# Hand-over between two fused graph networks: the last residual sums of the first network go to other buffers and its last steps to later places

## The chip, the cores and the metric

The kernel runs on one core of a Trainium2 chip. The metric is the device time of one execution in microseconds (us). Before the change it is 1732.25 us, the median of three runs (1732.20 to 1734.21).

## The reference

`x` holds 128 graphs of 64 nodes with 384 features (8192 rows), `adj` the 128 adjacency matrices of 64 x 64. Two networks run one after the other, each of two layers, and each is closed by a residual sum and a layer norm without gain:

```
x = layernorm(x + L0(x, adj))      # gated network
x = layernorm(x + L1(x, adj))      # softmax network

L0, per layer: u = h Wl' h' (row >= column side) or h Wr' h' (other side), / sqrt(H)
               att = exp(u) * adj / (row sum + 1e-10);  ctx = att (h Wlin' + b)
               h = relu((ctx - mean) / (std + 1e-3) * a + b2)
L1, per layer: a = softmax(h h' / sqrt(H)) * adj, rows divided by their sums
               ctx = (a upper)(h Wl' + bl) + diag(a) (h Ws' + bs) + (a lower)(h Wr' + br)
               h = relu((ctx - mean) / sqrt(var + 1e-12) * g + beta)
```

Every product of TensorE is made of three: each operand is split into a high and a low part, and high x high, high x low and low x high are summed.

## The kernel before

**Tiling.** The rows are worked off in 8 passes of two streams (s = 0, 1); a stream is four tiles of 128 rows, and a tile holds two graphs. A pass has four units: unit 0 and 1 are layer 0 of stream 0 and 1, unit 2 and 3 are layer 1 of stream 0 and 1. The first network does its 8 passes and writes its result to the array `x1` in HBM, then the second does its 8 from there. Each engine has its own instruction list, in an order written out by hand; semaphores are the only link, so an instruction that waits holds everything behind it on its engine. The first and the last pass of each network are unrolled, and the unrolled last pass of the first network already starts the second one.

**A unit of the second network.** TensorE folds the scores (`fold_parts`, L1128 and L1131), computes twelve value products V0 to V11 (`values`, L1155, nine matmuls each, in a ring of four PSUM banks), the scores of the next unit (L119) and the contexts (L1168). V_j with j mod 3 below 2 needs its bank to be seeded with the bias by ScalarE (`seed`, L1254), and the seed needs the bank to have been read by VectorE (`biased_value` of job j-4, L1492 or L1496; for V0 and V1 of the first unit of all, `context_stats` of the first network, L761). ScalarE copies the high parts (`value_hi`, L1260), VectorE subtracts the low parts. In units 2 and 3 TensorE also transposes the exponentials (L1139), and while units 1 and 2 run it transposes the rows of units 2 and 3 (`turn_block`, L1112).

**The hand-over.** The results of the last units of the first network stand in `z[0]` and `z[1]`. For both streams there are still to come, in this order: gain and shift (`gain_and_shift`, VectorE L793 and L796), the residual sum (`add_residual`, L803, z and x_res to z), the row statistics of the sum (`final_stats` L808, `final_var` L812 to L817), the power -0.5 on GpSimd (`final_roots`, L634), the offset (`final_offset`, L821), the normalisation on ScalarE (`final_normalise`, L509) and the store to `x1` on the SP queue (`store_last`, L312). Before the change this stands at:

- stream 0: residual sums and statistics in VectorE's last `up_to_contexts` of the first network, ahead of `context_stats`; the roots on GpSimd ahead of the gated roots of stream 1; the four normalisations (`gated_normalise(0)`) in ScalarE's list of unit 0, between `seed` 6 and `value_hi` 3; the store on SP, ahead of the first weights of the second network's second layer (L1049).
- stream 1: gain and shift, sum and statistics in VectorE's list of units 0 and 1; roots on GpSimd in unit 0; normalisations on ScalarE in the second half of unit 1.

Layer 1's weights of the second network (three, staged in the second network's `x_res` buffers) are split in high parts (`weight_hi`, ScalarE L1207) and low parts (`weight_lo`, GpSimd L1371). The third one is loaded once the first is split, and the first rows `x_res` of the second network once all three are.

Of the kernel before, what the change touches and what calls it, by code (L numbers as in the profile page):

```python
# [123 lines left out]
def gated_layers(nc, ctx, sh, x, x_t, adj, adj_t, w_left, w_right, w_lin_t, b_lin, ln_a, ln_b, table, x1,  # L124
# [26 lines left out]
    with ExitStack() as overlaid:  # L151
# [14 lines left out]
        x_res1 = late("x_res1", [P, NT, H])  # L166
# [16 lines left out]
        x_res = [sb("x_res0", [P, NT, H]), x_res1]  # L183
# [66 lines left out]
        def sync_program(sp):  # L250
# [91 lines left out]
            def store_last(s):  # L342
                store_x1(PASSES - 1, s)
# [104 lines left out]
        def scalar_program(act):  # L448
# [136 lines left out]
            def last_normalise(s):  # L585
                final_normalise(PASSES - 1, s)
# [105 lines left out]
        def vector_program(dve):  # L692
# [151 lines left out]
            def up_to_contexts(i, unit, last, s):  # L844
# [23 lines left out]
                if not more:  # L868
                    add_residual(i, s)
# [3 lines left out]
                if more:  # L873
                    query_lo(i, unit + 1, 0)
                context_stats(i, unit, 0, more)
                if s is not None:
                    final_stats(i, s, NT - 1)
                context_stats(i, unit, 1, more)
                if s is not None:
                    final_var(i, s)  # L880
                context_stats(i, unit, 2, more)
                context_stats(i, unit, 3, more)
# [18 lines left out]
            class Tail:  # L901
# [12 lines left out]
                @staticmethod  # L914
                def residual_and_stats(tiles):
                    add_residual(*end, tiles)
                    for t in tiles:
                        final_stats(*end, t)

                @staticmethod  # L920
                def final_var():
                    final_var(*end)

                @staticmethod
                def final_offset():
                    final_offset(*end)
# [6 lines left out]
def softmax_layers(nc, ctx, sh, gated, x1, adj_t, w_nbr_t, table, out):  # L933
# [26 lines left out]
    with ExitStack() as block_ctx:  # L960
# [84 lines left out]
        def _(sp):  # L1045
# [15 lines left out]
            store_last(0)  # L1061
# [4 lines left out]
            store_last(1)  # L1066
            sp.wait_ge(split, SIDES)

            def one_pass(i, last):
# [21 lines left out]
            one_pass(0, False)  # L1091
# [109 lines left out]
        def _(act):  # L1201
# [84 lines left out]
            def second_half(i, unit, more, tail):  # L1286
# [11 lines left out]
                if tail:  # L1298
                    gated_normalise(1)
# [7 lines left out]
                if tail:  # L1307
                    weight_hi(2)
                if more:
                    copy_part(i, unit + 1)  # L1310

            def one_pass(i, last, first=False):

                for unit in range(UNITS):
                    more = not (last and unit == UNITS - 1)
                    if more:
# [7 lines left out]
                        second_half(i, unit + 1, not (last and unit == UNITS - 2), first and unit == 0)  # L1324
# [18 lines left out]
            gated_normalise(0)  # L1343
# [3 lines left out]
            weight_hi(0)  # L1347
# [9 lines left out]
            copy_part(0, 1)  # L1357
            weight_hi(1)
# [6 lines left out]
        def _(pool):  # L1365
# [49 lines left out]
            def one_pass(i, last, first=False):  # L1415

                for unit in range(UNITS):
# [3 lines left out]
                    if first and unit == 0:  # L1421
# [327 lines left out]
```

## Time and profile before

| what | value |
|---|---|
| median of three runs | 1732.25 us |
| profiled execution, its own time | 1731.75 us |
| its span | 1730.2 us |
| granted TensorE clock, mean | 0.993 |
| TensorE matmul busy | 1672.8 us, 97% |
| VectorE, ScalarE, GpSimd busy | 1268.5, 949.1, 614.5 us |

All places in the trace are us from the start of the span. The first network ends and the second begins at about 848 us. PE is TensorE's matmul stream, DVE VectorE, ACT ScalarE, POOL GpSimd, SPq the queue of the SP engine. In rows of a timeline the bracket gives how long the engine sat idle before the piece and what released it.

### The profile page before, as it was taken

The page shows a single profiled execution, that of the slowest core. Times are in us where ns is not written, and L with a number is a line of the kernel's source. Part 1 is how long each engine was busy: PE and PEld are TensorE (multiplying, and loading weights), DVE is VectorE, ACT ScalarE, POOL GpSimd, SP SyncE. Part 2 cuts the span into 40 slices and gives each one's busy share as a digit, 9 for nine tenths or more (in the row PEclk, how much of TensorE's full clock was granted, in tenths as well). Part 3 has the DMA queues.
Part 4 walks back from the last instruction along what each step waited for, and adds up shares of the span by engine and source line. Part 5 has one row for each costly group of instructions (what it writes and reads, how often), then busy time and mean ns, then how long its engine had stood idle before and what let it go on. Part 6 is the DMA issues. An engine that isn't in the chain of part 4 may idle for free.

```text
span 1730.2 us, 29842 instructions
## 1 busy us (share of the span) xinstructions
PE 1672.8 (97%) x9664; PEld 1577.8 (91%) x9664; DVE 1268.5 (73%) x2785; ACT 949.1 (55%) x1985; POOL 614.5 (36%) x658
## 2 busy tenths in 40 slices
PE   7999999999999999999889999999999999999994
PEld 6989989889888989989889999999999999999994
DVE  4587685867769587686876968768687686877866
ACT  4545455364554645456466565565664656656553
POOL 5143252433324243253422514334153351523503
PEclk9999999999999999999999999999999999999997
DMA  7015021020300212013023040400304003030201
GB/s 228 1 31 155 6 66 56 24 91 6 115 6 24 91 30 91 6 53 80 4 78 77 22 94 18 99 0 22 94 21 95 0 26 90 21 95 0 67 11 37
DMA packets 108015, 92.19 MB, mean 53 GB/s; under 512 B 63280, under 2 KB 101168, under 8 KB 107952
## 3 DMA queue, kind: packets, MB, share of 16 engines
q1 hardware_dynamic: 107952, 91.51, 18.5%
q8 instruction: 20, 0.33, 0.1%
q14 instruction: 43, 0.35, 0.1%
HBM read 66.33 MB, written 25.17 MB: 53 GB/s over the span
## 4 chain that ended last, share of the span: by engine, by line
PE 46%; issue 33%; POOL 10%; DVE 6%; ACT 2%; SPq 1%; DMA 1%; POOLq 0%; DVEq 0%; ACTq 0%
PE b_work L1155 30%; PE b_work L1168 6%; POOL g_qv_lo L621 3%; POOL b_ht L601 3%; PE b_score_ps L119 2%; PE b_work L372 2%; PE b_score_ps L386 1%; PE b_work L396 1%; PE b_turn L1112 1%; POOL g_keep_l L616 1%; POOL g_sigma L630 1%; POOL g_a_nat L617 1%; DVE b_z L1530 1%; POOL g_frstd L634 1%; DVE b_ht L1466 1%
## 5 line engine op out<-in xcount | busy, mean ns | idle before, releaser
L1155 PE MATMUL b_work<-b_w_hi,b_ht 128*128 128x384 f32 x2304 | 609.7, 339 | 13.6 <-ACT b_work L1254 13.6
L1155 PEld LDWEIGHTS b_work<-b_w_hi,b_ht 128*128 128x128 f32 x2304 | 418.6, 188 | 18.4 <-ACT b_work L1254 17.8
L1155 PE MATMUL b_work<-b_w_lo,b_ht 128*128 128x384 f32 x1152 | 385.8, 335 | 0.0
L372 PE MATMUL b_work<-b_ht,b_w_hi 128*128 128x512 f32 x1152 | 357.7, 392 | 9.8 <-DVE b_w_lo L696 9.8
L372 PEld LDWEIGHTS b_work<-b_ht,b_w_hi 128*128 128x128 f32 x1152 | 216.2, 189 | 51.5 <-issue 9.7
L621 POOL TENSOR_TENSOR g_qv_lo<-g_v_full,g_qv_hi 128x384 fp32r<-128x384 f32 x128 | 133.4, 1062 | 361.0 <-ACT g_qv_hi L495 361.0
L372 PE MATMUL b_work<-b_ht,b_w_lo 128*128 128x512 f32 x576 | 225.8, 392 | 0.0
L1492 DVE TENSOR_TENSOR s_v_lo<-b_work,s_v_hi 128x384 fp32r<-128x384 f32 x256 | 139.3, 554 | 108.4 <-ACT s_v_hi L1260 107.5
L1155 PEld LDWEIGHTS b_work<-b_w_lo,b_ht 128*128 128x128 f32 x1152 | 217.1, 188 | 0.0
L728 DVE TENSOR_TENSOR g_qv_lo<-b_work,g_qv_hi 128x512 fp32r<-128x512 f32 x192 | 128.7, 687 | 110.8 <-ACT g_qv_hi L483 108.9
L396 PE MATMUL b_work<-b_w_hi,b_ht 128*128 128x384 f32 x768 | 206.3, 336 | 0.0
L1254 ACT ACTIVATE b_work<-b_bias 128x384 f32<-128x384 f32 x256 | 126.4, 494 | 128.9 <-DVE b_z L1530 82.0
L483 ACT ACTIVATE g_qv_hi<-b_work 128x512 fp32r<-128x512 f32 x192 | 110.5, 591 | 131.8 <-PE b_work L372 131.8
L1260 ACT ACTIVATE s_v_hi<-b_work 128x384 fp32r<-128x384 f32 x256 | 121.3, 488 | 56.5 <-PE b_work L1155 55.6
L386 PE MATMUL b_score_ps<-g_qv_hi,b_ht 128*128 128x256 f32 x768 | 146.9, 285 | 4.5 <-DVE g_qv_lo L728 4.5
L396 PEld LDWEIGHTS b_work<-b_w_hi,b_ht 128*128 128x128 f32 x768 | 139.8, 188 | 1.2
L372 PEld LDWEIGHTS b_work<-b_ht,b_w_lo 128*128 128x128 f32 x576 | 108.7, 189 | 23.1
L396 PE MATMUL b_work<-b_w_lo,b_ht 128*128 128x384 f32 x384 | 128.6, 335 | 0.0
L386 PEld LDWEIGHTS b_score_ps<-g_qv_hi,b_ht 128*128 128x128 f32 x768 | 120.5, 188 | 8.2 <-DVE g_qv_lo L728 7.1
L1396 POOL TENSOR_TENSOR s_rstd<-s_var,s_power 128x4 f32<-128x4 f32 x32 | 32.2, 1007 | 237.1 <-DVE s_var L1549 237.1
L487 ACT ACTIVATE g_prob<-g_score_l 128x512 f32<-128x512 f32 x32 | 20.2, 632 | 164.6 <-DVE g_score_l L740 164.6
L386 PE MATMUL b_score_ps<-g_qv_lo,b_ht 128*128 128x256 f32 x384 | 107.1, 279 | 0.0
(138 smaller groups left out, 3247.7 us busy)
## 6 DMA issues: line engine op xcount, KB each, us to landing
b_x_in<-in_x_t SPq DMA_DIRECT2D x16, 768.0 KB, 6.9
g_x_res<-in_x SPq DMA_DIRECT2D x16, 768.0 KB, 7.6
x<-b_z SPq DMA_DIRECT2D x16, 768.0 KB, 3.9
b_x_in<-x SPq DMA_DIRECT2D x64, 192.0 KB, 6.7
s_x_res<-x SPq DMA_DIRECT2D x16, 768.0 KB, 6.9
out<-b_z SPq DMA_DIRECT2D x15, 768.0 KB, 4.1
b_a_tr<-in_adj_t SPq DMA_DIRECT2D x64, 64.0 KB, 3.4
g_a_nat<-in_adj SPq DMA_DIRECT2D x32, 64.0 KB, 2.4
```

The costliest lines, as they stand in the source:

```text
L372: mm = pe.matmul(bank[:], w, h, start=(n == 0), stop=(n == len(pairs) - 1))
L386: mm = pe.matmul(score_ps[:, t, :, :], h, q, start=(n == 0), stop=(n == len(pairs) - 1))
L396: mm = pe.matmul(bank[:, 0:H], h, w, start=(n == 0), stop=(n == len(pairs) - 1))
L483: nc.scalar.activation(q_hi[:, m, :, d, :], work[use % RING][:], ACT.Copy).then_inc(q_hi_ready, 1)
L601: nc.gpsimd.tensor_tensor(ht_lo[s][:, k, :], xt_in[s][:, k, :], ht_hi[s][:, k, :].bitcast(F32), ALU.subtract).then_inc(x_split, 1)
L621: nc.gpsimd.tensor_tensor(v_lo[:, t, 0:H], v_full[:, t, :], v_hi[:, t, 0:H].bitcast(F32), ALU.subtract).then_inc(v_lo_ready, 1)
L728: op = nc.vector.tensor_tensor(q_lo[:, m, :, d, :], bank, q_hi[:, m, :, d, :].bitcast(F32), ALU.subtract)
L1155: mm = pe.matmul(bank[:, 0:H], h, w, start=(n == 0 and side == 2), stop=(n == len(pairs) - 1), skip_group_check=True)
L1168: mm = pe.matmul(bank[:, 0:HC], p, v, start=(n == 0), stop=(n == len(pairs) - 1))
L1254: nc.scalar.activation(work[(unit * WN + j) % RING][:, 0:H], bias[:, side, layer_of(unit), :], ACT.Copy)\
L1260: nc.scalar.activation(v_hi[:, t, side, 0:H], work[(unit * WN + j) % RING][:, 0:H], ACT.Copy)\
L1492: nc.vector.tensor_tensor(v_lo[:, t, side, 0:H], bank[:, 0:H], v_hi[:, t, side, 0:H].bitcast(F32), ALU.subtract).then_inc(work_free, 1)
```

## The change

The residual sums of the last pass of the first network are written into `x_res[s]` in place of `z[s]`, so `x_res[0]`, like `x_res[1]`, stays allocated after the first network. Statistics, normalisations and stores of that pass read `x_res[s]`. The second network's first contexts no longer wait for the store of `z[s]` (`contexts_out(..., first=True)`). The steps move:

- VectorE: out of the last `up_to_contexts` of the first network go the four residual sums and all statistics of stream 0, and `context_stats` follow directly. Unit 0 has now: residual sums of stream 0 (behind `biased_value` 1, 3, 5's transposition and 10) and gain and shift of tiles 0 and 1 of stream 1 in place of all four; unit 1: gain and shift of tiles 2 and 3 and the four sums of stream 1; unit 2: all eight statistics, both variances, offset of stream 0; between unit 2 and 3: offset of stream 1.
- GpSimd: final roots of stream 0 go from ahead of `gated_roots` to unit 2's time, those of stream 1 likewise one later; all three `weight_lo` now stand in the loop's first unit, behind `diagonal(0, 1)`.
- ScalarE: the normalisations of stream 0 go to the end of unit 2's list, those of stream 1 to the end of unit 3's, each behind `copy_part`; `weight_hi(0)` goes from the middle of unit 0 to its end, `weight_hi(2)` from ahead of unit 1's `copy_part` to behind it.
- SP: the two stores go into the first pass, behind `load_adj(1, s)`; the loads of the first two weights are issued as soon as the first fold is done.

```diff
-        x_res1 = late("x_res1", [P, NT, H])
+        x_res = [late(f"x_res{s}", [P, NT, H]) for s in range(STREAMS)]
...
             def store_last(s):
-                store_x1(PASSES - 1, s)
+                sp.wait_ge(x1_ready, (PASSES - 1) * (STREAMS * NT) + NT * (s + 1))
+                sp.dma_start(x1_v[PASSES - 1, s], x_res[s][:]).then_inc(stored[s], 16)
...
             def last_normalise(s):
-                final_normalise(PASSES - 1, s)
+                act.wait_ge(foffset_ready, (PASSES - 1) * STREAMS + s + 1)
+                for t in range(NT):
+                    nc.scalar.activation(x_res[s][:, t, :], x_res[s][:, t, :], ACT.Identity, scale=frstd[s][:, t:t + 1],
+                                         bias=foffset[s][:, t:t + 1]).then_inc(x1_ready, 1)
...
                 if not more:
-                    add_residual(i, s)
+                    for t in range(NT):
+                        context_stats(i, unit, t, more)
+                    return
...
-                def residual_and_stats(tiles):
+                def residual(s, t):
+                    dve.wait_ge(res_loaded[s], 16 * PASSES)
+                    dve.wait_ge(scaled, (PASSES - 1) * (STREAMS * NT) + s * NT + t + 1)
+                    nc.vector.scalar_tensor_tensor(x_res[s][:, t, :], z[s][:, t, 0:H], 0.0, x_res[s][:, t, :],
+                                                   ALU.max, ALU.add).then_inc(summed, 1)
...   SP
-            store_last(0)
             load_weight(0)
             load_weight(1)
             sp.wait_ge(split, 1)
             load_weight(2)
-            store_last(1)
...
+                    if first:
+                        store_last(s)
...   ScalarE, second_half
-                if tail:
-                    gated_normalise(1)
...
-                if tail:
-                    weight_hi(2)
                 if more:
                     copy_part(i, unit + 1)
+                if tail == 1:
+                    weight_hi(2)
+                if tail in (2, 3):
+                    gated_normalise(tail - 2)
...   ScalarE, unit 0
-            gated_normalise(0)
             value_hi(0, 0, 3)
             value_hi(0, 0, 4)
             seed(0, 0, 7)
-            weight_hi(0)
...
             copy_part(0, 1)
+            weight_hi(0)
             weight_hi(1)
...   GpSimd
                     if first and unit == 0:
+                        weight_lo(0)
+                        weight_lo(1)
                         weight_lo(2)
...
+                    if first and unit == 1:
+                        gated_final_roots(0)
...
-            gated_final_roots(0)
             gated_roots()
...   VectorE, up_to_contexts of the second network (tail is the unit in the first pass)
+                    if tail == 1 and j < 5:
+                        gated.gain_and_shift(j - 1)
+                    if tail == 2:
+                        gated.final_stats(0, j - 3)
...
+                if tail == 1:
+                    gated.residual(1, 2)
+                if tail == 2:
+                    gated.final_offset(0)
+                    gated.final_stats(1, 0)
+                    gated.final_stats(1, 1)
...
+                if tail == 2:
+                    gated.final_stats(1, 2)
+                    gated.final_stats(1, 3)
+                    gated.final_var(1)
...
-                contexts_out(i, unit)
+                contexts_out(i, unit, tail == 1)
```

## Rows read from the trace of the kernel before

**Rows 1.** The page's busy times of the whole span.

```profile
PE 1672.8 (97%) x9664; PEld 1577.8 (91%) x9664; DVE 1268.5 (73%) x2785; ACT 949.1 (55%) x1985; POOL 614.5 (36%) x658
```

**Rows 2.** Waits of PE from 840 to 1000 us: total, times, longest.

```profile
PE b_work L1155 <- ACT b_work L1254: 8.2, 3, 3.2
PE b_turn L1112 <- DVE b_ht L1466: 1.6, 2, 1.4
PE b_work L407 <- POOL g_qv_lo L621: 0.8, 2, 0.5
```

**Rows 3.** Chain that ended last, in order of time: start, us, what.

```profile
884.50 12.57 PE b_work L1155 x72
...
912.57 6.32 PE b_work L1155 x36
...
939.92 6.32 PE b_work L1155 x36
946.24 0.44 PE b_turn L1139 x4
...
965.48 18.79 PE b_work L1155 x108
```

**Rows 4.** Timeline of PE around the hand-over: start, us, instruction, idle before.

```profile
850.98 0.69 PE L1155 MATMUL b_work<-b_w_hi,b_ht 128*128 128x384 f32 x1 [2.93 <-ACT b_work L1254]
...
865.97 0.45 PE L1155 MATMUL b_work<-b_w_hi,b_ht 128*128 128x384 f32 x1 [2.06 <-ACT b_work L1254]
...
872.58 0.44 PE L1155 MATMUL b_work<-b_w_hi,b_ht 128*128 128x384 f32 x1 [3.19 <-ACT b_work L1254]
```

**Rows 5.** Timeline of ACT, same stretch.

```profile
847.46 0.49 ACT L504 ACTIVATE b_z<-b_work 128x386 f32<-128x386 f32 x1 [0.66 <-PE b_work L407]
850.43 0.49 ACT L1254 ACTIVATE b_work<-b_bias 128x384 f32<-128x384 f32 x1 [2.48 <-DVE g_stats L761]
...
861.93 2.49 ACT L509 ACTIVATE b_z<-b_z,g_foffset,g_frstd 128x384 f32<-128x384 f32 x4
...
870.60 1.16 ACT L1207 ACTIVATE b_w_hi<-s_x_res 128x1152 fp32r<-128x1152 f32 x1 [4.68 <-DMA s_x_res<-in_L_gnn_Wl]
```

**Rows 6.** Timeline of DVE, the four sums of stream 0.

```profile
843.80 4.74 DVE L803 SCALAR_TENSOR_TENSOR b_z<-b_z,g_x_res 128x384 f32<-128x384 f32 x4
```

**Rows 7.** Lines L803 and L793 over the whole run: ns min/median/max, first and last start.

```profile
L803 DVE SCALAR_TENSOR_TENSOR b_z<-b_z,g_x_res x64: 537/552/1637, 108.2 to 887.5; 128x384 f32<-128x384 f32 x64
L793 DVE SCALAR_TENSOR_TENSOR b_z<-b_z,g_mv,g_gain x64: 607/616/1661, 98.2 to 867.0; 128x384 f32<-128x384 f32 x64
```

**Rows 8.** Timeline of POOL: one pass earlier, then at the hand-over.

```profile
738.68 3.05 POOL L621 TENSOR_TENSOR g_qv_lo<-g_v_full,g_qv_hi 128x384 fp32r<-128x384 f32 x3
...
842.91 3.65 POOL L621 TENSOR_TENSOR g_qv_lo<-g_v_full,g_qv_hi 128x384 fp32r<-128x384 f32 x3
846.53 4.37 POOL L1381 TENSOR_TENSOR s_keep<-b_a_tr,b_const 128x512 f32<-128x512 f32 x3
...
856.14 3.79 POOL L1381 TENSOR_TENSOR s_keep<-b_a_tr,b_const 128x512 f32<-128x512 f32 x3
```

**Rows 9.** Stretches: length, busy PE, PEld, DVE, ACT, POOL, granted clock, DMA share, GB/s.

```profile
850.98:854.30 3.32, 3.32 (x11) 3.32 (x11) 3.07 (x18) 2.43 (x11) 1.56 (x2) 0.51 0.00 0
869.40:872.58 3.18, 0.00 (x0) 0.00 (x1) 0.92 (x2) 1.98 (x4) 0.74 (x1) 1.00 0.68 252
853.58:877.87 24.29, 18.73 (x102) 17.48 (x100) 18.41 (x37) 12.12 (x24) 9.36 (x9) 0.99 0.30 98
913.40:936.20 22.80, 22.58 (x140) 22.19 (x139) 12.74 (x31) 15.70 (x36) 4.49 (x4) 1.00 0.53 107
```

**Rows 10.** Timelines of DVE and ACT at the end of unit 2.

```profile
936.21 0.62 DVE L1530 SCALAR_TENSOR_TENSOR b_z<-s_v_own,s_own,b_work 128x385 f32<-128x385 f32 x1 [1.88 <-PE b_work L1168]
...
936.86 0.50 ACT L1254 ACTIVATE b_work<-b_bias 128x384 f32<-128x384 f32 x1 [1.01 <-DVE b_z L1530]
```

**Rows 11.** DMA issue of the third weight: count, KB each, us to landing.

```profile
s_x_res<-in_L_gnn_Ws SPq DMA_DIRECT2D x1, 576.0 KB, 3.9
```

More of the change, by code:

```diff
@@ L1065, in _, with one_pass @@
             load_weight(2)
-            store_last(1)
             sp.wait_ge(split, SIDES)
-            def one_pass(i, last):
+            def one_pass(i, last, first=False):
                 for s in range(STREAMS):
@@ L1089, in one_pass @@
                         sp.dma_start(out_v[i, s], z[s][:, :, 0:H]).then_inc(stored[s], 16)
-            one_pass(0, False)
+            one_pass(0, False, first=True)
             with sp.Fori(1, PASSES - 1) as i:
@@ L1323, in one_pass @@
                         seed(i, unit + 1, 7)
-                        second_half(i, unit + 1, not (last and unit == UNITS - 2), first and unit == 0)
+                        second_half(i, unit + 1, not (last and unit == UNITS - 2), unit + 1 if first else None)
                     else:
@@ L1420, in one_pass @@
                     roots(i, unit)
-                    if first and unit == 0:
+                    if first and unit == 2:
                         gated_final_roots(1)
@@ L1518, in own_probability, with contexts_out @@
                 nc.vector.tensor_reduce(own[:], expo[:], AX.X, ALU.add).then_inc(own_ready, 1)
-            def contexts_out(i, unit):
+            def contexts_out(i, unit, first=False):
                 layer, s = divmod(unit % UNITS, STREAMS)
-                if layer == 0:
+                if layer == 0 and not first:
                     dve.wait_ge(stored[s], before[s] + 16 * (i + unit // UNITS))
@@ L1600, in final_normalise, with up_to_contexts @@
                                             ALU.mult, ALU.add).then_inc(last_ready, 1)
-            def up_to_contexts(i, unit, last, s):
+            def up_to_contexts(i, unit, last, s, tail=None):
                 more = not (last and unit == UNITS - 1)
@@ L1630, in up_to_contexts @@
                 biased_value(i, unit, 11)
+                if tail == 1:
+                    gated.residual(1, 3)
+                if tail == 2:
+                    gated.final_stats(1, 2)
+                    gated.final_stats(1, 3)
+                    gated.final_var(1)
                 if s is not None:
@@ L1648, in one_pass @@
                             biased_value(i, unit + 1, j)
-                            if first and unit == 0 and j == 0:
-                                gated.residual_and_stats((3,))
-                                gated.final_var()
                         deviations(i, unit)
-                        if first and unit == 0:
-                            gated.final_offset()
-                        up_to_contexts(i, unit + 1, last, s if layer == 1 else None)
+                        if first and unit == 2:
+                            gated.final_offset(1)
+                        up_to_contexts(i, unit + 1, last, s if layer == 1 else None, unit + 1 if first else None)
                     else:
@@ L1672, in _ @@
             biased_value(0, 0, 1)
-            gated.gain_and_shift(0)
+            gated.residual(0, 0)
             biased_value(0, 0, 2)
-            gated.gain_and_shift(1)
             nc.vector.memset(v_own[:, :, H:H + 1], 1.0)
@@ L1679, in _ @@
             biased_value(0, 0, 3)
-            gated.gain_and_shift(2)
+            gated.residual(0, 1)
             biased_value(0, 0, 4)
-            gated.gain_and_shift(3)
             flip_block(0, 1, 0)
@@ L1685, in _ @@
             flip_block(0, 1, 1)
+            gated.residual(0, 2)
             biased_value(0, 0, 6)
-            gated.residual_and_stats((0,))
+            gated.gain_and_shift(0)
             biased_value(0, 0, 7)
```

41 lines of the change are left out of this document (22 added, 19 removed).

## Prediction

> **What bounds the kernel now.** I read the page's busy times first, then the waits of PE, the chain in order of time, and the timelines of the four engines between 840 and 970 us. TensorE is busy for 97% of the span [rows 1]: outside the hand-over there is almost nothing to gain, and whatever keeps PE idle in it is paid in full, because 15 units of back-to-back products follow. In the hand-over PE waits three times for a bias seed of ScalarE, 8.2 us in all, and twice for a low part of GpSimd, 0.8 us [rows 2]. The yardstick is a unit without a stop. V0 of unit 3 starts at 939.92 and that of the next unit at 965.48, so 25.56 us, of which 0.44 are the transposed exponentials that layer 0 does not have: 25.1 us for a unit of layer 0 such as units 0 and 1 [rows 3]. Unit 2 lasts 939.92 - 912.57 = 27.35 us; less the 0.44 of exponentials, 26.9 us is the yardstick for unit 1, which like it carries the three transposed blocks [rows 3]. Unit 0 begins at 850.98 [rows 4]; the chain counts its starts 0.17 later (a matmul's pipelined end), so it lasts 884.50 - 851.15 = 33.35 us, and unit 1 lasts 912.57 - 884.50 = 28.07 us. The kernel before thus loses 8.25 us in unit 0 and 1.2 us in unit 1, and in addition starts V0 late.
>
> **Ahead of V0.** The first seed starts at 850.43, after ScalarE idled 2.48 us for the first statistics of the context [rows 5]. VectorE stood in four residual sums from 843.80 to 848.54 [rows 6] and three statistics behind them. The change takes both away, so the seed waits only for ScalarE's own copies of the contexts, the last of which ends at 847.95 [rows 5]. A second gain comes with it: those sums took 4.74 us where their median is 0.552 each, 2.2 us for four [rows 6, 7], and GpSimd beside them took 3.65 us for three low parts where one pass earlier it took 3.05, and 4.37 us for three masks where the next three took 3.79 [rows 8]. They slowed each other. Without them the third low part is ready 0.6 us sooner, the last context copy ends at about 847.35, and the masks end at 845.9 + 3.8 = 849.7 instead of 850.9. PE starts a seed's length (0.49) and a hop after 847.35, less what the ring hides: some 847.75. V0 moves from 850.98 to 847.75: **3.2 us**. The bounds are 2.5 (no gain from GpSimd) and 3.6.
>
> **Unit 0.** The two later stops are both ScalarE's order. The stop of 2.06 us before V7 [rows 4] comes from seed 7, which stands behind the four normalisations (2.49 us) [rows 5]; the one of 3.19 before V9 from seed 9, behind the split of the first weight, which waited 4.68 us for its DMA [rows 5], whose transfer SP had issued only after the store of stream 0. Both steps leave unit 0's middle. That is 5.25 us, and about 0.3 for each restart (a first matmul of 0.44 [rows 4] instead of a step of 18.79 / 108 = 0.174 us [rows 3]). The rest of the 8.25 is the clock: after the long stop the granted clock was 0.51, the lower level of 1.2 GHz, for 3.32 us, in which 11 matmuls ran that at the full level take 1.9 us: 1.4 us [rows 9]. What is late next? VectorE. In this stretch, from its first product with the masks to its last low part of unit 1's rows, it was busy 18.41 of 24.29 us [rows 9]. The new list has there one gain and shift in place of four (-3.6 us at 1.2 a pair, by two of the size in [rows 7]), one statistic less (-0.5) and two sums more (+1.1), so 15.4 us. It starts when the masks are there, 849.7; 1.9 us of waits for high parts stay (the split of products waits 1.0 us for ScalarE at the start, and 0.9 at job 3); it ends at 867.0. PE has done V11 at 847.75 + 18.8 = 866.5. So PE stops for some 0.6 us before the scores of unit 1, and 0.1 us around V5; with restarts of 0.3 unit 0 lasts 25.1 + 1.0 = 26.1 us, not 33.35: **7.2 us**. Bounds: 5.5 (VectorE late by 2 more) and 8.2 (nothing lost).
>
> **Unit 1.** The four normalisations of stream 1 stood ahead of the copies of the transposed blocks. They leave, `weight_hi(2)` (1.16 us [rows 5]) goes behind `copy_part`, where ScalarE waits for VectorE's contexts anyway; PE needs the third weight for V2 of unit 2, 3 us after the low part is done. The loss of 1.2 us goes down to about 0.3, since VectorE has now 2.4 us of gain and shift and 2.2 of sums in place of one sum, a statistic and its variance: **0.9 us**, bounds 0 and 1.2.
>
> **Units 2 and 3.** VectorE gets eight statistics, two variances and an offset, about 8 x 0.48 + 1.5 = 5.4 us. It has 22.80 - 12.74 = 10.1 us idle between unit 2's start and its contexts [rows 9], but 2.8 us of them come in the last stretch, where it idles 1.88 [rows 10]; its contexts start 0.9 us late. ScalarE gets four normalisations, 2.5 us, from 935.85 (where its idle time before 936.86 begins [rows 10]): it seeds V0 at 938.4 instead of 936.9, and V0 is due at 939.92. Hidden, with 1 us to spare; the transposition of the exponentials is 0 to 0.2 us late. At the end of unit 3 ScalarE idles 3.3 us before its seed, room for the 2.5 of stream 1. I put **-0.3 us**, bounds -2.5 and 0. SP's stores and GpSimd's roots have no one behind them who is due: the adjacency load of stream 1 behind the first store waited for the output of stream 0 before too.
>
> **Two-input operations.** In units 0 and 1 VectorE's sums and gains now stand beside GpSimd's masks and six of its weight subtractions (1.0 us each). What that costs is seen in the sums: 1.19 instead of 0.55 us [rows 6, 7], so +0.63 for each that meets one. Of the sums and gains I count four or five that do, 3 us of VectorE's time, and most of it in unit 1 where 19.9 - 13.9 = 6 us were idle; I charge **-0.6 us** and keep 0 and -3 as ends. The Trainium skill (SBUF - State Buffer, section "SBUF: two separate sides") states a rule that speaks against the change: VectorE's operations with two SBUF inputs and GpSimd's that read SBUF share one pair of ports as a lock, held for a whole instruction, the loser standing still. The trace agrees, in the 4.74 and 4.37 us; by the rule at its worst every one of the meetings would wait a whole instruction, and VectorE would be 4 to 5 us later.
>
> **Sum.** 3.2 + 7.2 + 0.9 - 0.3 - 0.6 = 10.4 us off the profiled execution (span 1730.2, own time 1731.75), to 1721.35. That execution lies 0.5 us under the median of 1732.25, so the median is forecast at 1732.25 - 10.4 = 1721.9, or -0.6%.
>
> **The rivals.**
> *VectorE becomes the bound of units 0 and 1.* The lag of 0.6 us before unit 1's scores shows that it is close; if it meets GpSimd more often, or the new sums stand ahead of low parts for which a bank is due, 3 to 4 us are lost: 1725.5. For it: 15.4 us of work in 17.3. Against: in unit 1 it has 6 us of idle time. 14%.
> *The lower clock comes all the same.* The clock fell after the stop of 2.93 us, but stayed at 1.00 over one of 3.18 us [rows 9], so the length of a stop alone does not decide. If the low stretch stays, 1.4 us are not won: 1723.3. 12%. The Trainium skill (TensorE: Matmul & The Clock Gate, "What's actually happening") says the gate has two levels and follows how busy the engine has been; both rows bear out the levels, and the second one shows that idle time need not lower it.
> *Units 2 and 3 give back.* If the late contexts and the normalisations of ScalarE add up instead of lying beside each other, V0 of unit 3 is 1 to 2.5 us late, and of the next unit likewise: 1724.5. 8%.
> *Slower: the third weight.* Its transfer is issued when GpSimd has split the first weight, and that split now stands behind unit 1's diagonal; ScalarE waits for the transfer ahead of all seeds of unit 2. By my timeline the low part ends at 882.5 and the transfer, 3.9 us [rows 11], at 886.5; ScalarE comes to it at 898 and needs 1.2 us, and V0 of unit 2 is due at 901.5. So a landing after 900 stops PE, one at 911 (24 us late) eats the gain, and one 35 us late gives 1743. Against it: nothing in their queues ahead is longer than 1.3 us. 3%.
> *The change does nothing,* since PE's stops are only moved to the same seeds: VectorE's second statistic held the second seed as well. Against it is the order itself; 3%, 1732.
>
> **How the numbers follow.** The forecast has 60%, the five rivals 40%. Its own range is 1719.8 to 1723. The far ends of the terms are 3.6 + 8.2 + 1.2 = 13.0 us (1719.3) and 2.5 + 5.5 + 0 - 2.5 - 3 = 2.5 us (1729.7), which will not all meet; 1719.5 to 1726.5 takes in the first three rivals and leaves out less than 2 in 10. A measurement of this kernel can tell 0.2%, 3.5 us, from no change: faster by more 0.93, within 0.04, slower 0.03.
>
> **What would show it.** PE's first matmul of L1155 at 847.5 to 848.5 with an idle time under 0.7; no stop over 1 us in unit 0, and one of about 0.6 before L119; granted clock 1.00 between 848 and 860; V0 of unit 1 at about 873.9, of unit 2 at 901 to 901.5; L1381's first three at 3.8 us; the last normalisations of ScalarE between `copy_part` and the seeds of units 3 and 4, with no stop of PE behind them. I am wrong if PE stops over 1 us for low parts of VectorE in units 0 or 1 (first rival), or V0 of unit 3 comes later than 27.6 us after that of unit 2 (third).

## Result and profile after

The kernel after takes 1723.28 us (median, 1723.0 to 1723.86), the kernel before, run beside it, 1733.23 us (1732.2 to 1734.6). The ratio is 0.9945, 95% interval 0.9933 to 0.9957: 9.5 us or 0.55% faster (the medians differ by 10.0). The forecast was 1721.9 us and "faster by over 0.2%"; the time lies 1.4 us above it and inside the range. The profiled execution has a span of 1722.1 us and an own time of 1723.86 us, 8.1 and 7.9 us under the one of before; it is the slowest of after's four runs, while that of before lies a little under its median. What follows explains the 8.1 us of the two profiles. (Lines below the gated network's functions have moved: L1155 is L1165 now, L1254 L1264, L1466 L1476, L1496 L1506, L1530 L1540, L1381 L1390, L621 L624, L817 L820.)

The page's busy times, which answer to [rows 1]: TensorE is 2.6 us less busy, the other engines do the same work.

```profile
PE 1670.2 (97%) x9664; PEld 1575.5 (91%) x9664; DVE 1267.1 (74%) x2785; ACT 950.2 (55%) x1985; POOL 613.1 (36%) x658
```

The waits of PE from 840 to 1000 us (total us, times, longest), which answer to [rows 2]: 8.2 us of waits for bias seeds have become 1.5, those for low parts and transposed blocks 1.0 instead of 2.4.

```profile
PE b_work L1165 <- ACT b_work L1264: 1.5, 2, 1.2
PE b_turn L1122 <- DVE b_ht L1476: 0.8, 3, 0.3
PE b_work L407 <- POOL g_qv_lo L624: 0.2, 1, 0.2
```

The chain in order of time (start, us, what), against [rows 3]. All of unit 0 is one piece of 108 matmuls; unit 1's V0 follows at 874.09, unit 2's at 901.32, the first matmul behind the new stop in unit 3 at 934.59, the next unit's V0 at 955.66.

```profile
848.13 19.35 PE b_work L1165 x108
...
874.09 4.77 PE b_work L1165 x27
...
901.32 6.32 PE b_work L1165 x36
...
934.59 1.84 PE b_work L1165 x9
936.43 0.44 PE b_turn L1149 x4
936.86 12.49 PE b_work L1165 x72
...
955.66 18.79 PE b_work L1165 x108
```

The timeline of PE (start, us, instruction, idle before): of the three stops of [rows 4], the first of them ahead of V0, only 0.34 us ahead of V0 is left. One of 0.32 us waits for a transposed block in unit 1 (1.41 us before), and a new one of 1.16 us stands in unit 3, ahead of V3.

```profile
848.13 0.44 PE L1165 MATMUL b_work<-b_w_hi,b_ht 128*128 128x384 f32 x1 [0.34 <-ACT b_work L1264]
...
891.22 0.66 PE L1122 MATMUL b_turn<-b_const,b_z 128*128 128x128 f32 x4 [0.32 <-DVE b_ht L1476]
...
934.59 0.44 PE L1165 MATMUL b_work<-b_w_hi,b_ht 128*128 128x384 f32 x1 [1.16 <-ACT b_work L1264]
```

The timelines of ACT and of POOL at the start, against [rows 5, 8]: the first seed follows the last context copy at once, 2.84 us earlier (847.59 against 850.43), and GpSimd's operations have lost their company: the three low parts take 3.03 us instead of 3.65, the three masks 3.76 instead of 4.37.

```profile
847.20 0.49 ACT L504 ACTIVATE b_z<-b_work 128x386 f32<-128x386 f32 x1 [0.33 <-PE b_work L407]
847.59 0.90 ACT L1264 ACTIVATE b_work<-b_bias 128x384 f32<-128x384 f32 x2
```

```profile
843.28 3.03 POOL L624 TENSOR_TENSOR g_qv_lo<-g_v_full,g_qv_hi 128x384 fp32r<-128x384 f32 x3
846.27 3.76 POOL L1390 TENSOR_TENSOR s_keep<-b_a_tr,b_const 128x512 f32<-128x512 f32 x3
```

Stretches (length, busy PE, PEld, DVE, ACT, POOL, granted clock, DMA share, GB/s), of after and then of before. The clock is 1.00, the upper level, over the hand-over, where before it was 0.51 for 3.32 us [rows 9]. The second row and the row of before are the same work, five passes of the second network's loop between the same two instructions: 535.48 us against 533.35. **Here 2.1 us are lost that the prediction does not know.**

```profile
846.00:860.00 14.00, 13.64 (x77) 12.85 (x77) 11.59 (x27) 8.65 (x26) 10.14 (x10) 1.00 0.26 85
1060.00:1595.48 535.48, 525.70 (x3162) 518.18 (x3161) 397.07 (x921) 311.95 (x741) 193.22 (x201) 1.00 0.19 47
```

```profile
1070.03:1603.38 533.35, 525.64 (x3163) 518.41 (x3161) 397.94 (x921) 311.54 (x741) 193.22 (x201) 1.00 0.19 47
```

**The account.** A unit is counted from its V0 to the next unit's V0. At the V0 that follows unit 3 the kernel is 965.48 - 955.66 = 9.82 us ahead:

- 2.85 from V0's start (850.98 to 848.13);
- 7.39 from unit 0 (874.09 - 848.13 = 25.96 against 33.35), and 0.17 from the way in which the chain counted unit 0's start before;
- 0.84 from unit 1 (27.23 against 28.07), nothing from unit 2 (27.36 against 27.35);
- 1.42 given back in unit 3 (26.98 against 25.56).

Behind it 1.7 us more go: 2.13 in the loop, less 0.4 won outside it.

Two losses thus had to be explained, and both begin on VectorE. **The first, in unit 3.** Timelines of DVE, POOL and ACT at the end of unit 2, against [rows 10]:

```profile
915.83 0.16 DVE L820 TENSOR_TENSOR g_fvar<-g_fvar,g_fmv 128x4 f32<-128x4 f32 x1
...
925.45 1.13 DVE L820 TENSOR_TENSOR g_fvar<-g_fvar,g_fmv 128x4 f32<-128x4 f32 x1
926.51 0.60 DVE L1540 SCALAR_TENSOR_TENSOR b_z<-s_v_own,s_own,b_work 128x385 f32<-128x385 f32 x1
```

```profile
922.76 3.81 POOL L1390 TENSOR_TENSOR s_keep<-b_a_tr,b_const 128x512 f32<-128x512 f32 x3 [5.68 <-DVE s_own L1528]
```

```profile
924.63 2.51 ACT L588 ACTIVATE g_x_res<-g_x_res,g_foffset,g_frstd 128x384 f32<-128x384 f32 x4
927.15 0.50 ACT L1264 ACTIVATE b_work<-b_bias 128x384 f32<-128x384 f32 x1
...
932.64 0.37 ACT L1251 ACTIVATE s_expo<-b_score_ps,s_exp_bias 128x128 f32<-128x128 f32 x1 [3.89 <-DVE s_exp_bias L1494]
```

The last operation of the variance, 128x4, takes 0.16 us for stream 0 and 1.13 for stream 1, and it ends (926.58) when GpSimd's third mask ends (922.76 + 3.81 = 926.57). The contexts of unit 2 start 926.51 - 901.32 = 25.19 us after its V0; before it was 936.21 - 912.57 = 23.64 [rows 3, 10], so they are 1.55 us late. ScalarE's exponentials wait 3.89 us for VectorE's bias, and the seed behind them stops PE. A rival explanation was that ScalarE's four normalisations, 2.51 us ahead of the seeds, make the stop.

**The second, in the loop.** Timeline of DVE in the pass that follows the loop's first jump back, of after and then of before. Both stop for 2.2 to 2.4 us at the same place; the profile shows no semaphore that they wait for ("issue"). After has a second stop some 1.7 us of work later.

```profile
1091.55 0.17 DVE L1549 SCALAR_TENSOR_TENSOR s_total<-s_exp_sum,b_z 128x4 f32<-128x4 f32 x1 [2.39 <-issue]
...
1093.99 0.56 DVE L1506 TENSOR_TENSOR s_v_own<-b_work,b_bias 128x384 f32<-128x384 f32 x1 [0.74 <-issue]
```

```profile
1101.42 0.17 DVE L1539 SCALAR_TENSOR_TENSOR s_total<-s_exp_sum,b_z 128x4 f32<-128x4 f32 x1 [2.23 <-issue]
...
1103.04 0.55 DVE L1496 TENSOR_TENSOR s_v_own<-b_work,b_bias 128x384 f32<-128x384 f32 x1
```

After each of the five jumps back the second stop is there in after, 0.63 to 0.90 us, 3.8 us in all; before has one of 0.19 us in all five passes. PE waits for seeds there, from 1085 to 1560 us, ten times in after and five in before (total us, times, longest), first after and then before:

```profile
PE b_work L1165 <- ACT b_work L1264: 7.5, 10, 1.3
```

```profile
PE b_work L1155 <- ACT b_work L1254: 5.4, 5, 1.2
```

These 2.1 us are the 2.13 of the stretches. They are a difference: the five units with the jump are 3.3 us longer in after (28.9 to 29.2 us each instead of 28.4 to 28.6), and 1.2 us come back elsewhere, because before has another stop without a releaser in each pass that after has not. It costs PE 0.2 us a time (a unit of 25.8 us instead of 25.55). Waits of DVE from 1070 to 1604 us in before:

```profile
DVE s_row_max L1482 <- issue: 1.6, 5, 0.3
```

**What moves in these stops.** The only transfers from 1088 to 1096 us are three of the queue that carries instructions. Rates in 40 slices of 0.2 us, and the queue (packets, MB, share), of after:

```profile
GB/s 0 0 0 0 0 0 0 41 0 0 0 0 0 0 0 0 0 0 0 0 41 0 0 0 0 0 0 0 0 0 0 0 41 0 0 0 0 0 0 0
q14 instruction: 3, 0.02, 1.1%
```

The trace has these three packets, of 8 KB each, after every jump back of every kernel here. The first stop ends 1.3 to 1.5 us after the first packet has landed, the second stop 1.25 to 1.45 us after the second. That fits VectorE waiting for its own instructions in both stops; the trace doesn't say for which engine a packet is.

Theory: where the second stop falls, and how long it is, follows from where VectorE's instructions stand in its list. Rival: a wait of the hand-over that goes on through the passes.

**How many instructions the change adds.** The page counts 2785 for VectorE in both kernels, but it leaves out the waits for semaphores that stand as instructions of their own. Those at the first network's residual sums (engine, operation, times: ns, first to last start) are 19 in before and 14 + 8 = 22 in after, since `residual` waits twice per tile; by the trace's records all other counts of VectorE are equal. **VectorE's list is three instructions longer in after, all ahead of the loop.** First before, then after:

```profile
L802 DVEq EVENT_SEMAPHORE  x19: 21/21/21, 107.4 to 887.0; - x19
```

```profile
L805 DVEq EVENT_SEMAPHORE  x14: 21/21/21, 108.0 to 757.6; - x14
L921 DVEq EVENT_SEMAPHORE  x8: 21/21/21, 854.1 to 895.1; - x8
```

### The profile page after: what moved, and what is told of

Its sections match the earlier page's. It is cut to its first block, busy times and chain, and to the rows that moved or that the text cites. A ratio compares the mean times of both kernels' runs of the same rounds, so it can differ in the third digit from the quotient of the medians.

```text
span 1722.1 us, 29844 instructions
## 1 busy us (share of the span) xinstructions
PE 1670.2 (97%) x9664; PEld 1575.5 (91%) x9664; DVE 1267.1 (74%) x2785; ACT 950.2 (55%) x1985; POOL 613.1 (36%) x658
## 4 chain that ended last, share of the span: by engine, by line
PE 44%; issue 34%; POOL 11%; DVE 6%; ACT 3%; SPq 1%; DMA 0%; POOLq 0%; DVEq 0%; ACTq 0%
PE b_work L1165 29%; PE b_work L1178 6%; POOL g_qv_lo L624 3%; POOL b_ht L604 3%; PE b_work L372 2%; PE b_score_ps L119 2%; PE b_score_ps L386 1%; PE b_work L396 1%; POOL g_keep_l L619 1%; DVE b_z L1540 1%; PE b_turn L1122 1%; POOL g_sigma L633 1%; POOL g_a_nat L620 1%; POOL g_frstd L637 1%; ACT b_turn L1229 1%
## 5 line engine op out<-in xcount | busy, mean ns | idle before, releaser
L1165 PE MATMUL b_work<-b_w_hi,b_ht 128*128 128x384 f32 x2304 | 608.2, 338 | 9.0 <-ACT b_work L1264 9.0
L1165 PEld LDWEIGHTS b_work<-b_w_hi,b_ht 128*128 128x128 f32 x2304 | 417.5, 188 | 13.5 <-ACT b_work L1264 12.9
L1165 PE MATMUL b_work<-b_w_lo,b_ht 128*128 128x384 f32 x1152 | 385.2, 334 | 0.0
L624 POOL TENSOR_TENSOR g_qv_lo<-g_v_full,g_qv_hi 128x384 fp32r<-128x384 f32 x128 | 132.8, 1057 | 360.9 <-ACT g_qv_hi L495 360.9
L1165 PEld LDWEIGHTS b_work<-b_w_lo,b_ht 128*128 128x128 f32 x1152 | 216.5, 188 | 0.0
L1264 ACT ACTIVATE b_work<-b_bias 128x384 f32<-128x384 f32 x256 | 126.2, 493 | 126.7 <-DVE b_z L1540 76.3
```

The source lines that it names most:

```text
L624: nc.gpsimd.tensor_tensor(v_lo[:, t, 0:H], v_full[:, t, :], v_hi[:, t, 0:H].bitcast(F32), ALU.subtract).then_inc(v_lo_ready, 1)
L1165: mm = pe.matmul(bank[:, 0:H], h, w, start=(n == 0 and side == 2), stop=(n == len(pairs) - 1), skip_group_check=True)
L1264: nc.scalar.activation(work[(unit * WN + j) % RING][:, 0:H], bias[:, side, layer_of(unit), :], ACT.Copy)\
```

## Experiments

Where no interval stands, a time is that of a single run with a profile, and its profile's rows are the evidence, not its time; other times are medians. "Before" is the kernel before, run beside it. In the cuts of code, steps are shortened to what changes.

### The statistics of stream 1 behind unit 2's contexts (kernel after)

```diff
 up_to_contexts(i, unit, last, s, tail)
-    if tail == 2:
-        gated.final_stats(1, 2)
-        gated.final_stats(1, 3)
-        gated.final_var(1)
 one_pass(...)
     maximum(i, unit + 1)
+    if first and unit == 2:
+        gated.final_stats(1, 2)
+        gated.final_stats(1, 3)
+        gated.final_var(1)
```

> The changed kernel with the last two statistics and the variance of stream 1 moved from ahead of unit 2's contexts into unit 3, behind the row maximum, where VectorE idled 2.37 us. Theory: the 1.16 us stop of PE in unit 3 is made on VectorE, whose contexts of unit 2 start 1.55 us late (25.19 us after V0 of unit 2 instead of 23.64); with the steps gone the contexts start at about +23.7, the stop goes, unit 3 lasts 25.5 instead of 26.98 us from fold to fold, and the kernel gains 1.3 to 1.5 us on the changed one (0.9945 of before becomes about 0.9937). Rival: the stop comes from ScalarE's four normalisations ahead of unit 3's seeds; then it stays and unit 3 still lasts 27.0 us.

Measured: 1721.55 us (5 runs, 1721.25 to 1721.73), before 1732.58; ratio 0.9936 [0.9922, 0.9950]. PE has no stop over 0.3 us in unit 3, which lasts 25.56 us (counted here and below from PE's last fold ahead of a unit to the last one ahead of the next, 927.43 to 952.99), as in before. Timeline of DVE: the contexts start 23.65 us after V0 of unit 2 again, as PE delivers them.

```profile
924.28 0.62 DVE L1540 SCALAR_TENSOR_TENSOR b_z<-s_v_own,s_own,b_work 128x385 f32<-128x385 f32 x1 [0.89 <-PE b_work L1178]
```

The normalisations stay on ScalarE where they were, so the rival is out: the stop came from the steps that VectorE had ahead of the contexts. The second stop of the loop is still there (0.60 to 0.69 us each, at L1506).

### The variance's last operation with one input (kernel after)

```diff
-nc.vector.tensor_tensor(fvar[:], fvar[:], fmv[:, :, 1], ALU.add)
+nc.vector.tensor_scalar(fvar[:], fmv[:, :, 1], 1e-5, None, ALU.add)
```

> The changed kernel, with the last operation of the hand-over's variance (add of two 128x4 tiles in SBUF, 1.13 us where it took 0.16 for stream 0) written as an add of a constant to one tile, at the same place, same count of instructions. Theory: it stood still because it has two inputs in SBUF while GpSimd made masks from 922.8 to 926.6; with one input it takes 0.1 to 0.2 us, the contexts of unit 2 start 1.0 us earlier (+24.2 after V0 of unit 2), and PE's stop of 1.16 us in unit 3 shrinks to 0 to 0.3. Rival: the amount of VectorE work is the cause (eight statistics, two variances); then the operation still ends at about +25.2 and the stop stays over 0.9 us.

Measured: 1723.27 us, and the stop is there. Timelines of DVE, POOL and PE:

```profile
925.11 1.16 DVE L939 TENSOR_SCALAR g_fvar<-g_fmv 128x4 f32<-128x4 f32 x1
```

```profile
922.42 3.82 POOL L1397 TENSOR_TENSOR s_keep<-b_a_tr,b_const 128x512 f32<-128x512 f32 x3 [5.68 <-DVE s_own L1535]
```

```profile
934.26 0.44 PE L1172 MATMUL b_work<-b_w_hi,b_ht 128*128 128x384 f32 x1 [1.17 <-ACT b_work L1271]
```

My theory falls as to the form: an operation with one SBUF input waits just as long, and again ends with the third mask (925.11 + 1.16 = 926.27; 922.42 + 3.82 = 926.24). The Trainium skill (SBUF - State Buffer, "SBUF: two separate sides") names two sorts of VectorE operations that take the pair of ports shared with GpSimd: those with two SBUF inputs, and those in a mode that uses both ports. That this `tensor_scalar` ran in such a mode agrees with its 1.16 us, but no run here shows the mode itself.

### The masks of pass 1 a unit later (kernel after)

```diff
-if not last and unit % STREAMS == 1:
+if not last and unit % STREAMS == 1 and not (first and unit == 1):
     masks(i + 1, unit // STREAMS)
+if first and unit == 2:
+    masks(i + 1, 0)
```

> The changed kernel with GpSimd's masks for stream 0 of the next pass (3.8 us, L1390) moved in the first pass from the end of unit 2 to unit 3, behind its own gains and shifts, so that nothing of GpSimd runs beside the hand-over's second variance. Theory: that variance's last operation took 1.13 us (and 1.16 with one input in SBUF) because it stood still until the third mask was done at 926.57; alone it takes 0.16 to 0.2 us, unit 2's contexts start at +24.1 to +24.3 us after V0 of unit 2 instead of +25.2, and PE's stop of 1.16 us in unit 3 falls below 0.4 us. Rival: it waited for something else, such as the statistics in front of it; then it still takes 1.1 us and the stop stays.

Measured: 1721.56 us, before 1732.24. Timeline of DVE: without GpSimd beside it the same two-input operation takes 0.16 us, and the contexts start 24.2 us after V0 of unit 2, 1.0 us earlier than in after.

```profile
924.85 0.16 DVE L820 TENSOR_TENSOR g_fvar<-g_fvar,g_fmv 128x4 f32<-128x4 f32 x1
924.94 0.62 DVE L1542 SCALAR_TENSOR_TENSOR b_z<-s_v_own,s_own,b_work 128x385 f32<-128x385 f32 x1
```

PE's stop falls from 1.16 to 0.22 us; unit 3 lasts 26.08 us (927.50 to 953.58). So about 0.9 of the 1.42 us are GpSimd's masks, and 0.5 the added steps themselves, behind which the contexts still start 0.6 us later than in before.

### One part alone: stream 0's statistics behind the gated ones (kernel before)

```diff
 if not more:
+    for t in range(NT):
+        context_stats(i, unit, t, more)
     add_residual(i, s)
+    for t in range(NT):
+        final_stats(i, s, t)
+    final_var(i, s)
+    final_offset(i, s)
+    return
```

> The kernel before, with one thing changed: in VectorE's last list of the first network the four context statistics come first, then the residual sums, statistics, variance and offset of stream 0 (at their old buffers). Theory: V0 of unit 0 comes 2.5 to 3.2 us earlier (847.8 to 848.5 in place of 851.0), the low clock of 3.3 us does not come; but 8 us of VectorE work now stand ahead of the products with the masks, so V4 to V6 of unit 0 stop for their seeds for 4 to 6 us, and V0 of unit 1 comes 0 to 2 us later than before: 1731 to 1735 us. Rival: the sums are hidden behind PE's four first jobs; then all of it is kept, 1728 to 1729 us.

Measured: 1734.53 us (10 runs), ratio 1.0013 [1.0004, 1.0022]: slower by a hair. Timelines of PE and DVE:

```profile
847.54 0.45 PE L1162 MATMUL b_work<-b_w_hi,b_ht 128*128 128x384 f32 x1 [0.34 <-ACT b_work L1261]
...
858.90 0.69 PE L1162 MATMUL b_work<-b_w_hi,b_ht 128*128 128x384 f32 x1 [4.84 <-ACT b_work L1261]
...
867.66 0.44 PE L1162 MATMUL b_work<-b_w_hi,b_ht 128*128 128x384 f32 x1 [1.59 <-ACT b_work L1261]
...
874.28 0.69 PE L1162 MATMUL b_work<-b_w_hi,b_ht 128*128 128x384 f32 x1 [3.21 <-ACT b_work L1261]
```

```profile
847.61 3.52 DVE L803 SCALAR_TENSOR_TENSOR b_z<-b_z,g_x_res 128x384 f32<-128x384 f32 x4
```

V0 starts 3.4 us earlier than before, as in the change, and all of it is given back behind one new stop of 4.84 us: V0 of unit 1 comes 2.4 us later than in before, where 0 to 2 were expected. The sums and statistics now stand ahead of the value products, whose banks the next seeds need. The low clock, which was expected to stay away, came twice, behind the stops of 4.84 and 3.21 us. The gain ahead of V0 is worth something only if that work does not go into unit 0's first third.

### The other part alone: weights ahead of the store, the split behind the scores (kernel before)

```diff
-x_res1 = late("x_res1", [P, NT, H])
+x_res = [late(f"x_res{s}", [P, NT, H]) for s in range(STREAMS)]
...
-store_last(0)
 load_weight(0)
 load_weight(1)
+store_last(0)
...
-weight_hi(0)
 value_hi(0, 0, 6)
...
 copy_part(0, 1)
+weight_hi(0)
 weight_hi(1)
```

> The kernel before, with only the weight steps of the change: both loads ahead of the store of stream 0 on SP, the split of the first weight at the end of ScalarE's list of unit 0, and x_res of stream 0 kept after the first network (else the second load would overwrite it). Theory: PE's stop of 3.19 us before V9 goes, that of 2.06 before V7 stays, V0 of unit 1 comes 2.5 to 3.5 us earlier and the kernel takes 1729 to 1730 us. Rival: VectorE is as late as ScalarE there (18.4 us of work), and most of the stop comes back before unit 1's scores: V0 of unit 1 less than 1.5 us earlier.

Measured: 1729.42 us (10 runs), ratio 0.9981 [0.9972, 0.9990]. Timeline of PE: the stop of 3.19 us is now 0.49, the one of 2.06 is 1.25, the one ahead of V0 stays.

```profile
850.81 0.69 PE L1154 MATMUL b_work<-b_w_hi,b_ht 128*128 128x384 f32 x1 [2.94 <-ACT b_work L1253]
...
865.77 0.44 PE L1154 MATMUL b_work<-b_w_hi,b_ht 128*128 128x384 f32 x1 [1.25 <-ACT b_work L1253]
...
869.67 0.44 PE L1154 MATMUL b_work<-b_w_hi,b_ht 128*128 128x384 f32 x1 [0.49 <-ACT b_work L1253]
```

From fold to fold unit 0 is 2.5 us shorter (33.98 against 36.45). The split of the first weight, which waited for its transfer, was the cause of the longest stop; this run moves both, and doesn't say which of the two would have been enough. Alone this part is worth 3.2 us of median, the other less than nothing, and the whole change 9.5. The whole is more than these two parts: it also takes the normalisations out of unit 0, behind which V7's stop stood, and spreads the sums and the work for stream 1. That these make up the rest is argued from the timelines; no run has them alone.

### Four small instructions more on VectorE (after, then before)

Four memsets of 128x1 on VectorE in the unrolled first pass, ahead of the loop; they do nothing. In after they stand ahead of unit 1's `contexts_out`, in before ahead of unit 1's `up_to_contexts`:

```diff
+scratch = sb("scratch", [P, 64])
...
+for k in range(4):
+    nc.vector.memset(scratch[:, k:k + 1], 1.0)
```

> The changed kernel with four tiny memsets (a scratch tile, 0.06 us each) in VectorE's list of the first pass, so that its loop of the second network stands four instructions later. At each of the five jumps back VectorE stops without a cause in the trace: 2.2 us in both kernels, and in the changed one again for 0.63 to 0.90 us two values later (five times, 3.8 us), where the kernel before has 0.19 once. Theory: the second stop hangs on where VectorE's instructions stand in memory; four more move it by four instructions (it appears earlier in the list, ahead of L1502, or in another size). Rival: it comes from something else of the changed kernel (buffers, other engines); then it stays at the same instruction with 0.6 to 0.9 us.

> The kernel before with the same four memsets. Theory of place: it now has a second stop of 0.5 to 1.0 us after each jump back and the five passes of the loop take 107.0 to 107.2 us instead of 106.7, without any part of the change. Rival: no second stop.

Measured: 1737.23 us for after, 14 more than without; 1738.13 for before, 6 more. Timelines of DVE in the first loop pass after a jump, of after with the memsets and of before with them:

```profile
1093.22 1.02 DVE L1503 TENSOR_TENSOR s_v_lo<-b_work,s_v_hi 128x384 fp32r<-128x384 f32 x2 [1.58 <-issue]
```

```profile
1105.72 0.56 DVE L1493 TENSOR_TENSOR s_v_lo<-b_work,s_v_hi 128x384 fp32r<-128x384 f32 x1 [1.00 <-issue]
```

In after the second stop lasts 1.58 to 1.78 us each time, and it comes four records earlier: counted from the jump back, with waits and register operations, it ends with VectorE's record 12, in after without the memsets with record 16. In before with four more it is record 15, one less than in after: four more instead of three. PE stops for 2.72 to 2.91 us each time, and the granted clock fell to its lower level at each of the five stops or up to 1.1 us behind it (the first matmul here takes 0.69 us instead of 0.44):

```profile
1094.36 0.69 PE L1166 MATMUL b_work<-b_w_hi,b_ht 128*128 128x384 f32 x1 [2.77 <-ACT b_work L1265]
```

The units with the jump last 31.6 to 32.8 us instead of 28.9 to 29.2. In before a second stop of 1.00 to 1.29 us appears that was not there, more than the 0.5 to 1.0 expected, and a pass takes 107.3 to 107.9 us. The loop makes 4.3 of its 6 us; about 2 come from the hand-over, where the stop before V9 is 3.24 us and is followed by the lower clock. In after all of the 14 us lie in the loop, which the four instructions of some 0.06 us do not touch. A wait of the hand-over would not come again at each of five jumps and move by as many records as there are instructions more: the rival is out.

### Two instructions less on VectorE (kernel after)

```diff
-nc.vector.memset(fvar[:], 1e-5)
 for t in range(NT): bn_aggr(...)
-nc.vector.tensor_tensor(fvar[:], fvar[:], fmv[:, :, 1], ALU.add)
+nc.vector.tensor_scalar(fvar[:], fmv[:, :, 1], 1e-5, None, ALU.add)
```

> The changed kernel with two memsets of VectorE's hand-over left out (the variance adds its constant itself), so that its loop stands two instructions earlier. Theory of place: the second stop after the jump back goes from L1506 two instructions on, where the kernel before had it at 0 to 0.2 us, and the five loop passes get 0.3 us shorter each, 1.5 to 2 us in all. Rival: it stays, 0.6 to 0.9 us at the same instruction.

Measured: 1721.02 us, span 1719.2. Timeline of DVE:

```profile
1091.05 0.17 DVE L1555 SCALAR_TENSOR_TENSOR s_total<-s_exp_sum,b_z 128x4 f32<-128x4 f32 x1 [2.23 <-issue]
...
1092.66 0.55 DVE L1512 TENSOR_TENSOR s_v_own<-b_work,b_bias 128x384 f32<-128x384 f32 x1
```

The second stop is nearly gone (0.31 us once, 0.16 once, over five passes, at record 18); a pass lasts 106.6 us, as in before. The stop of 1.15 us in unit 3 stays. Compare the one-input run, which has the memset still: there the stop in the loop is 0.60 to 0.88 us. It is the number of instructions, not the form. The two runs with one part each, whose parts only reorder VectorE's list of before, have no second stop over 0.23 us either.

### Both repairs together

The edit is the first and the last of the above.

> The changed kernel with both findings: the last two statistics and the variance of stream 1 in unit 3 behind the row maximum, and the variance without its memset, so that VectorE's loop stands two instructions earlier. If the two losses are separate (1.43 us in unit 3; five second stops, 107.1 to 106.6 us per pass), they add: the span is 1722.1 - 1.4 - 1.8 to 2.2 = 1718.5 to 1719 us without the differences of the start, the time 1719.5 to 1720.5 and the ratio to before 0.992 to 0.993. Rival: VectorE's later list makes unit 3 or the jump worse, then not below 1721.

Measured: 1720.19 us (5 runs, 1719.91 to 1720.94), before 1732.82 (9 runs); ratio 0.9928 [0.9914, 0.9942]. Unit 3 lasts 25.55 us (927.80 to 953.35) and a loop pass 106.6 to 106.8. This version is faster than before by 12.6 us and, by the ratios, than after by about 3. Each loss stays mended beside the other: both stretches are as short as in the run that mended one alone.

## Why the prediction was right, and where it was not

- **Ahead of V0, 3.2 us: right.** V0 came 2.85 us earlier in a profile whose first network ran 0.38 us later by then: 3.2. (ScalarE's split of a weight that was just loaded starts at 21.11 us there, at 20.60 in before; the change does not touch it.) Both parts of the argument show, the missing sums and GpSimd's shorter operations.
- **Unit 0, 7.2 us: right, 7.4.** All stops over 0.3 us inside it are gone and the clock stayed at its upper level. The stop of 0.6 us before unit 1's scores did not come: VectorE was less late than reckoned. The two runs with one part each show that neither is enough: from fold to fold 36.45 in before, 33.98 with the weights moved, 39.75 with the statistics moved, 26.30 in after. The 7.2 came from the yardstick of 25.1 us, not from the terms of the loss: 5.25 + 0.6 + 1.4 make 7.25, so "The rest of the 8.25 is the clock" does not come out. Part of the gap is a stop that the prediction does not name, 0.36 us ahead of unit 1's scores at 877.92.
- **Unit 1, 0.9 us: right, 0.84.**
- **Two-input operations, -0.6 us: too much in units 0 and 1, where PE lost nothing.** They did meet GpSimd: one gain took 1.10 and one shift 1.26 us where the next pair, 2.8 us later, took 0.60 and 0.62. VectorE had room. By the Trainium skill's rule at its worst VectorE would have been 4 to 5 us later; operations that meet are longer, but nothing due stood behind them. It cost where nothing was charged for it, in unit 2.
- **Units 2 and 3, -0.3 us: mechanism named, size wrong; it measured -1.4.** The step that failed is "its contexts start 0.9 us late" together with "the transposition of the exponentials is 0 to 0.2 us late". The contexts start 1.55 us late; V0 of unit 3 still comes in time (27.36 us after that of unit 2), but PE stops 1.16 us ahead of V3, just before the exponentials are transposed. The steps for stream 1 stand in the last stretch ahead of the contexts, just when GpSimd does three masks for the next pass, and the variance waits for the third of them. Taking these steps away takes PE's stop away, taking the masks away leaves 0.22 us of it, while ScalarE's four normalisations, the other half of the worry, were hidden as said. The loss has the size of the rival "units 2 and 3 give back" but not its way: late contexts and normalisations did not add up, and V0 of unit 3 was not late.
- **Not in the sum at all: -2.1 us in the loop.** The prediction held that outside the hand-over there is almost nothing to gain, and so put it at nothing. VectorE's second stop behind each jump back costs PE 0.4 us net in each of five passes. A few instructions more or fewer ahead of the loop do it, in either direction, and the runs line up by their number:

| VectorE instructions more than before | runs | second stop, us | record that it ends with |
|---|---|---|---|
| 0 | before, and the two with one part alone | 0 to 0.23 | not counted |
| 1 | after with two fewer, with and without the other repair | 0 to 0.31 | 18 |
| 3 | after, and its three variants of equal count | 0.60 to 0.90 | 16 |
| 4 | before with four more | 1.00 to 1.29 | 15 |
| 7 | after with four more | 1.58 to 1.78 | 12 |

Each instruction more moves the second stop forward by one record, while the packet that ends it lands at about the same time after the jump. So VectorE comes to the end of the instructions that it has earlier, and waits longer. That the three semaphore waits of the change alone make after's loss is not tested by a run that leaves them out, but the run with two memsets less shows that the count is enough.

The sum: 10.4 forecast; 9.8 found at the end of the hand-over; 8.1 over the spans. That the time came within 1.4 us of the forecast is in part luck: the 0.6 us charged for two-input operations was not lost, which hides about half of what unit 3 lost beyond the forecast, and the medians differ by 10.0 us where the two profiled executions differ by 8.1.

## What to carry to other kernels

Count idle time of an engine by the stretch ahead of the instruction that is due, not over a unit, and look at what GpSimd does in that stretch before putting a small VectorE operation there. When a change in unrolled code shifts the time of a loop that it does not touch, compare the stops with no releaser after the jump back and count semaphore waits as instructions: a second stop costs, and two instructions fewer ahead of the loop can remove it. A gain that only moves a wait ahead of a ring must be tried together with the part that keeps the ring going: of the two parts tried alone here, one was worth nothing and the other 3 us, the whole change 9.5.

## What the runs showed of the hardware

- VectorE stops for 2.17 to 2.48 us after each of the five jumps back of this loop, in all eleven kernels, and a second stop of 0 to 1.8 us follows, depending on the number of instructions ahead of the loop. Three 8 KB packets of the instruction queue, 2.4 to 2.7 us from the first to the second, go with each jump, and the stops end 1.25 to 1.5 us after a packet has landed. Four memsets, 0.06 us each, made the kernel 14 us slower through it.
- A `tensor_scalar` of 128x4 with one SBUF input took 1.16 us beside GpSimd's masks, as long as the two-input form (1.13); without them that form took 0.16.
- The clock does not follow the length of PE's stop alone: in the hand-over it fell at stops of 2.93 and 3.24 us, and of 3.21 in the run with the statistics moved, but not over one of 3.18 in the kernel before [rows 9]; in the loop of after with four memsets more it fell at each of five stops of 2.72 to 2.91 us or just behind it.
